# A five-stage decoder on one core: weights of three stages loaded, and of one rounded, a stage earlier, and one transfer per tile between stages

## The chip, the cores and the metric

The kernel runs on one core of a Trainium2 chip. The metric is the device time of the whole program in microseconds, as the median of the runs. The program is written in Bass: each engine (TensorE "PE", VectorE "DVE", ScalarE "ACT", GpSimd "POOL", SyncE "SP", which issues all transfers) has its own instruction stream, and the streams meet only at semaphores.

## What is computed

`x` is 2 sequences (B) of 2048 tokens (S) with 512 features (D). Six sublayers follow one another, each with a layer norm over the sum of its input and its output:

```
x = LN(x + delta_rule(x))            # 16 heads, short convolutions
x = LN(x + context_attention(x, c))  # 16 heads x 64, softmax over 128 context tokens
x = LN(x + ffn(x))                   # fake-quantised, below
x = LN(x + decaying_average(x))      # k, v, r products; running weighted average
x = LN(x + strided_attention(x, c))  # 16 heads over 8 strided context tokens each
x = LN(x + tree(x))                  # router products, 256 leaf probabilities, leaf values

def act_q(x, clip):  s = sigmoid(clip) * max|x| / 127; return clamp(round(x / s), -128, 127) * s
def w_q(w):          s = max|w| per row / 127;         return clamp(round(w / s), -128, 127) * s
def ffn(x):          xq = act_q(x, clip_x)
                     h = silu(xq @ w_q(gate).T) * (xq @ w_q(up).T)      # gate, up: 1408 x 512
                     return act_q(h, clip_down) @ w_q(down).T           # down: 512 x 1408
```

## The kernel before

The program runs five stages one after the other; every intermediate `x` lies in DRAM twice, as rows (`x`) and transposed, as columns (`xT`). `Memory`, the helper that owns a stage's buffers and semaphores, ends each stage with a barrier over all engines, so no instruction of a stage is issued before the stage ahead has stored everything.

- `delta_rule_attention`: not touched.
- `context_attention` (buffers `ctxatt_`): 16 steps of 128 tokens of both sequences, with a lag between the parts. In a step PE makes 8 units (2 heads each) of query products (L1249), scores (L1261), transposes of the probabilities (L1270), products with v (L1280), and then the output product (L1288) and the transposes of the new rows (L1295). DVE subtracts each row's maximum (`shift`, L1371 to L1374), ACT takes the exponential (L1330), DVE divides (`soften`, L1381 to L1383), ACT copies the transposed probabilities out of PSUM (L1335). SP's step is a fixed order of one column load, one row store, one row load and four column stores, each behind a wait.
- `quantised_feed_forward`, in three blocks. The hidden part (`ffnh_`) loads gate and up in four pieces, finds each row's maximum (L1569), scales (L1578, DVE), rounds by adding and taking away a large constant (L1665, ACT), clamps (L1583, DVE), transposes on PE (L1724), copies out of PSUM (`keep_piece`, L1673, ACT), and then runs over 8 tiles of 256 tokens of both sequences. Hidden values go to DRAM (`h`), since their scale needs the maximum over all of them. A short block (`ffns_`) turns the down weights. The last part (`ffnd_`) loads the hidden values again (L1826), scales them (L1872, DVE), rounds them, multiplies and norms.
- `decaying_average` (`wkv_`): 16 steps of 128 tokens, and `strided_attention_and_tree` (`tree_`), written out without loops. Both begin with the loads of their own weights.

What an engine does in a step is a Python function `step(n)`. `pipelined(...)` wraps it into a hardware loop, `unrolled(...)` writes all steps out. Transfers of SP are issued in program order, and a wait of SP holds up everything behind it:

```python
def step(n):                                   # SP, context_attention, before
    if n:
        wait(sp, projected, n, PAIRS // 2, -PAIRS // 2)
        ...
        sp.dma_start(xT_sb[:, n.parity]..., xT_view[n.slot()]...)                # L1184
    if t := n.back(LAG):
        wait(sp, norm.done, t, norm.OPS, norm.OPS)
        sp.dma_start(x_out_view[tokens(t)], new[:, t.parity])                    # L1190
    ...
    if t := n.back(LAG + 1):
        wait(sp, newT_kept, t, B, B)
        for k in range(KB):
            sp.dma_start(xT_out_view[:, k, :, tokens(t)], newT[:, t.parity, k])  # L1199
```

## Time and profile before

| | |
|---|---|
| median of 3 runs | 2984.55 us (2983.33 to 2997.24) |
| the profiled execution | 2985.33 us, of which the span of instructions is 2983.3 us |
| mean granted clock of TensorE | 0.939 of full speed |
| busy share of the span | PE 86%, PEld (weight loads) 61%, DVE 76%, ACT 48%, POOL 16% |
| moved | 233.95 MB, mean 78 GB/s |
| stage bounds (us from the span's start) | delta rule 0 to 1052.8, context attention to 1793.69, feed-forward hidden part to 2001, down weights turned by 2011.02, feed-forward last part to 2147.79, decaying average to 2698.76, strided attention and tree to 2983.3 |

The stage bounds are the starts of the first instructions behind each barrier in the timelines. Busy shares are means over stages with different limits: in the 740.89 us of context attention PE is busy for 703.64, in the first 30 us of the hidden part it is not busy at all. So each stage is read by itself, and for the start of a stage the timeline of its first microseconds on every engine.

In a row of the timeline the first number is the start (us from the span's start), the second the time from the first start to the last end of a run of like instructions, then engine, line, operation, out<-in by the names of the buffers, the shapes and the number of instructions (xN); in brackets stands how long the engine idled before the row, and what ended the idling. SPq is the time in which SP issues transfers.

### The profile page before, as it was taken

The page shows a single profiled execution, that of the slowest core. Times are in us where ns is not written, and L with a number is a line of the kernel's source. Part 1 is how long each engine was busy: PE and PEld are TensorE (multiplying, and loading weights), DVE is VectorE, ACT ScalarE, POOL GpSimd, SP SyncE. Part 2 cuts the span into 40 slices and gives each one's busy share as a digit, 9 for nine tenths or more (in the row PEclk, how much of TensorE's full clock was granted, in tenths as well). Part 3 has the DMA queues.
Part 4 walks back from the last instruction along what each step waited for, and adds up shares of the span by engine and source line. Part 5 has one row for each costly group of instructions (what it writes and reads, how often), then busy time and mean ns, then how long its engine had stood idle before and what let it go on. Part 6 is the DMA issues. An engine that isn't in the chain of part 4 may idle for free. (4 is left out here: it accounts for less than half of the span.)

```text
span 2983.3 us, 86333 instructions
## 1 busy us (share of the span) xinstructions
PE 2574.6 (86%) x35332; PEld 1821.6 (61%) x35332; DVE 2252.7 (76%) x3969; ACT 1422.2 (48%) x2560; POOL 484.5 (16%) x661
## 2 busy tenths in 40 slices
PE   7789888988886679999999974987589989987998
PEld 5667666766665357667676642443276766764665
DVE  4999998999988217787777856978578778760787
ACT  7666666666762102223222225545355565541444
POOL 2233223323421100000000000006400000000122
PEclk9899999999997689999999996999799999998999
DMA  2001110111010140111101116519821211214342
GB/s 84 24 11 37 48 39 32 39 46 39 32 46 25 45 170 8 50 57 57 56 29 55 49 51 214 188 67 337 279 69 57 85 56 56 77 36 163 113 128 78
DMA packets 184030, 233.95 MB, mean 78 GB/s; under 512 B 21778, under 2 KB 106386, under 8 KB 183700
## 3 DMA queue, kind: packets, MB, share of 16 engines
q1 hardware_dynamic: 183700, 229.17, 23.4%
q8 instruction: 253, 4.15, 0.6%
q14 instruction: 77, 0.63, 0.1%
HBM read 136.32 MB, written 92.81 MB: 77 GB/s over the span
## 5 line engine op out<-in xcount | busy, mean ns | idle before, releaser
L718 ACT ACTIVATE delta_product<-delta_line,delta_conv_w 128x256 f32<-128x256 f32 x576 | 247.2, 498 | 0.2
L1249 PE MATMUL ctxatt_banks<-ctxatt_xT,ctxatt_wq 128*128 128x256 f32 x1024 | 232.4, 380 | 2.9 <-ACT ctxatt_qT L1325 2.1
L1288 PE MATMUL ctxatt_banks<-ctxatt_wo,ctxatt_oT 128*128 128x512 f32 x512 | 229.4, 601 | 4.9 <-DVE ctxatt_norm_y L1394 4.9
L1249 PEld LDWEIGHTS ctxatt_banks<-ctxatt_xT,ctxatt_wq 128*128 128x128 f32 x1024 | 189.7, 190 | 28.4 <-ACT ctxatt_qT L1325 3.3
L944 DVE TENSOR_TENSOR delta_squares<-delta_t_sys 128x30 f32<-128x30 f32 (+14 forms) x480 | 185.7, 387 | 12.9
L947 DVE TENSOR_TENSOR delta_t_sys<-delta_t_sys,delta_squares 128x30 f32<-128x30 f32 (+14 forms) x480 | 161.4, 336 | 16.6
L1288 PEld LDWEIGHTS ctxatt_banks<-ctxatt_wo,ctxatt_oT 128*128 128x128 f32 x512 | 95.8, 192 | 116.0 <-issue 109.5
L1335 ACT ACTIVATE ctxatt_probsT<-ctxatt_banks 128x512 f32<-128x512 f32 x128 | 69.4, 594 | 203.3 <-PE ctxatt_banks L1270 203.3
L455 POOL TENSOR_TENSOR delta_product<-delta_product 128x1024 f32<-128x1024 f32 x48 | 127.4, 2655 | 233.7 <-ACT delta_product L718 233.7
L2169 PE MATMUL wkv_banks<-wkv_woT,wkv_oT 128*128 128x512 f32 x256 | 130.0, 667 | 38.0 <-DVE wkv_oT L2367 38.0
L884 DVE TENSOR_TENSOR delta_conv<-delta_conv,delta_product 128x1024 f32<-128x1024 f32 x96 | 133.6, 1404 | 17.1 <-ACT delta_product L718 12.5
L1325 ACT ACTIVATE ctxatt_qT<-ctxatt_banks 128x512 f32<-128x512 f32 x64 | 38.2, 597 | 226.7 <-PE ctxatt_banks L1249 226.7
L2159 PE MATMUL wkv_banks<-wkv_mixed,wkv_wkT 128*128 128x256 f32 x512 | 118.4, 385 | 27.8 <-DMA wkv_wrT<-L_attn_wrT 27.8
L710 ACT ACTIVATE delta_conv<-delta_line,delta_conv_b,delta_conv_w 128x256 f32<-128x256 f32 x192 | 111.0, 595 | 64.8 <-DVE delta_v_tok L895 61.3
L532 PE MATMUL delta_banks<-delta_xT,delta_wkT 128*128 128x256 f32 x512 | 132.7, 404 | 10.2 <-ACT delta_line L700 6.9
L595 PE MATMUL delta_banks<-delta_woT,delta_oT 128*128 128x512 f32 x256 | 130.2, 656 | 12.6 <-DVE delta_norm_y L1001 10.9
L1388 DVE COPY ctxatt_oT<-ctxatt_banks 128x512 f32<-128x512 f32 x64 | 44.1, 689 | 117.4 <-PE ctxatt_banks L1280 117.4
L532 PE MATMUL delta_banks<-delta_xT,delta_wqT 128*128 128x256 f32 x512 | 130.3, 400 | 0.2 <-ACT delta_line L700 0.2
L532 PE MATMUL delta_banks<-delta_xT,delta_wvT 128*128 128x256 f32 x512 | 127.7, 394 | 0.7 <-ACT delta_line L700 0.7
L2159 PEld LDWEIGHTS wkv_banks<-wkv_mixed,wkv_wkT 128*128 128x128 f32 x512 | 98.0, 194 | 41.3 <-DMA wkv_wrT<-L_attn_wrT 28.2
L2169 PEld LDWEIGHTS wkv_banks<-wkv_woT,wkv_oT 128*128 128x128 f32 x256 | 53.4, 214 | 107.8 <-issue 93.9
L209 POOL TENSOR_TENSOR ctxatt_norm_var_eps<-ctxatt_norm_moments,ctxatt_eps 128x2 f32<-128x2 f32 x16 | 3.1, 194 | 714.8 <-DVE ctxatt_norm_moments L193 714.8
(341 smaller groups left out, 6301.4 us busy)
## 6 DMA issues: line engine op xcount, KB each, us to landing
h<-ffn_hid SPq DMA_DIRECT2D x66, 256.0 KB, 2.0
ffn_hid<-h SPq DMA_DIRECT2D x6, 1536.0 KB, 9.6
wkv_xT<-xT SPq DMA_DIRECT2D x64, 129.0 KB, 2.8
delta_xT<-xT SPq DMA_DIRECT2D x16, 512.0 KB, 5.1
delta_x<-x SPq DMA_DIRECT2D x16, 512.0 KB, 3.7
xT<-delta_newT SPq DMA_DIRECT2D x16, 512.0 KB, 2.9
x<-delta_new SPq DMA_DIRECT2D x16, 512.0 KB, 3.9
ctxatt_xT<-xT SPq DMA_DIRECT2D x16, 512.0 KB, 4.3
```

The costliest lines, as they stand in the source:

```text
L455: pool.tensor_tensor(two_taps, two_taps, last, ALU.add).then_inc(paired, 1)
L532: mm = pe.matmul(b_proj[:, p % 2, 0:B * P], wT[NAMES[i]][:, k, g * P:(g + 1) * P], xT_sb[:, n.parity, k], start=k == 0, stop=k == KB - 1)
L595: mm = pe.matmul(b_out, oT[:, g, b * P:(b + 1) * P], woT[:, g], start=g == 0, stop=g == KB - 1)
L710: act.activation(conv[:, i, g].rearrange("p (b t) -> p b t", b=B), line[:, i, g, :, 0:P], ACT.Identity, bias=conv_b[:, i, g:g + 1], scale= ...
L718: made = act.activation(slot(n, i)[:, j - 1, g].rearrange("p (b t) -> p b t", b=B), line[:, i, g, :, j:j + P], ACT.Copy, scale=conv_w[:, i ...
L884: c.did(dve.tensor_tensor(total, total, slot(n, i)[:, half_of].rearrange("p g n -> p (g n)"), ALU.add))
L944: c.did(dve.tensor_tensor(parts, t_sys[:, j + 1:, j:j + 1].to_broadcast([P, rows, j]), t_sys[:, j:j + 1, 0:j].to_broadcast([P, rows, j]), ...
L947: c.did(dve.tensor_tensor(to, to, parts, ALU.add))
L1249: mm = pe.matmul(b_q[:, i * B * P:(i + 1) * B * P], wq[:, k, pair * P:(pair + 1) * P], xT_sb[:, n.parity, k], start=k == 0, stop=k == KB - 1)
L1288: mm = pe.matmul(b_o[:], oT[:, b, k, :], wo[:, k, :], start=k == 0, stop=k == PAIRS - 1)
L2159: mm = pe.matmul(bank(i, q)[:, j * WCOLS:(j + 1) * WCOLS], mats[name][:, k, u * P:(u + 1) * P], mixed[:, n.parity, i, k].rearrange("p b t ...
L2169: mm = pe.matmul(banks[:, OUT_BANK + r], oT[:, n.parity, k, r * P:(r + 1) * P], mats["woT"][:, k], start=k == 0, stop=k == KB - 1)
```

## The change

1. Gate and up weights are loaded and rounded during context attention, 22 blocks of 128 x 512 in 11 pieces of two. SP's `load_piece` opens its steps 1 to 11; DVE's `scale_piece` opens its steps 2 to 12 and `clip_piece` its steps 4 to 14; ACT's `round_piece` opens its steps 3 to 13. The rounded blocks, their scales, the identity matrix, the maxima of the rows and the first columns for the feed-forward stay in SBUF (`RoundedWeights`). Step 15 of SP loads these columns. The hidden part then begins with the 88 transposes, gate and up blocks in turn; ACT copies the gate blocks out of PSUM, DVE the up blocks.
2. The weights of the decaying average (4 of 1 MB and five short vectors) are loaded in step 1 of SP in the feed-forward's last part, its first columns in step 9 (`DecayWeights`).
3. The first weights of the last stage (4 of 1 MB, the context, a mask, the identity and four short vectors) are loaded in step 2 of SP in the decaying average (`AttentionWeights`).
4. `xT` between the stages has another layout, so that a tile's columns go in one transfer and not in four.
5. The loops of SP, PE, ACT and DVE in context attention and of PE in the decaying average are written out, and not hardware loops.

```diff
 # context_attention, SP
                 def step(n):
+                    if 1 <= n.index <= PIECES:
+                        load_piece(n.index - 1)
                     if n:
                         wait(sp, projected, n, PAIRS // 2, -PAIRS // 2)
...
                         sp.sem_inc(passed, 1)
-                        for k in range(KB):
-                            sp.dma_start(xT_out_view[:, k, :, tokens(t)], newT[:, t.parity, k]).then_inc(newT_stored[t.parity], 16)
-
-                pipelined(sp, STEPS, LAG + 1, step)
-                sp.wait_ge(topped, STEPS)
-                sp.dma_start(top_out, tops[:]).then_inc(top_stored, 16)
+                        to = xT_out[t.index // 2, :, :, :, (t.index % 2) * P:(t.index % 2 + 1) * P]
+                        sp.dma_start(to.rearrange("p k b t -> p (k b) t"), newT[:, t.parity].rearrange("p k b t -> p (k b) t")).then_inc(newT_stored[t.parity], 16)
+                    if n.index == STEPS - 1:
+                        load_first_columns()
+
+                unrolled(sp, STEPS, LAG + 1, step)
...
+                def load_piece(q):
+                    if q >= 2:
+                        sp.wait_ge(w_rounded, 2 * (q - 1))
+                    for i, (k, b) in enumerate(blocks(q)):
+                        sp.dma_start(raw[:, q % 2, i], later.w[k].rearrange("(b p) n -> p b n", p=P)[:, b]).then_inc(raw_here[q % 2], 16)
 # context_attention, ACT
+                def round_piece(q):
+                    for i, (k, b) in enumerate(blocks(q)):
+                        act.wait_ge(w_scaled, 2 * q + i + 1)
+                        act.activation(later.whole[k][:, b], raw[:, q % 2, i], ACT.Identity, bias=minus_magic[:]).then_inc(w_rounded, 1)
                 def step(n):
                     t1, t2, t3 = n.back(1), n.back(2), n.back(3)
+                    if 0 <= n.index - 3 < PIECES:
...
+                        round_piece(n.index - 3)
 # context_attention, DVE
                 def step(n):
                     t1, t2, t3 = n.back(1), n.back(2), n.back(3)
+                    if 0 <= n.index - 2 < PIECES:
+                        scale_piece(n.index - 2)
+                    if 0 <= n.index - 4 < PIECES:
+                        clip_piece(n.index - 4)
 # quantised_feed_forward, hidden part, DVE and ACT in step 0
                         if first:
                             scale_x(n)
-                            round_weights()
+                            scale_outputs()
+                            keep_turned(range(8))
                             clip_x(n)
+                            keep_turned(range(8, IB))
...
                         if first:
+                            keep_turned(range(4))
                             round_x(n)
-                            for q in range(len(PIECES)):
-                                round_piece(q)
-                                if q > 0:
-                                    keep_piece(q - 1)
-                            keep_piece(len(PIECES) - 1)
+                            keep_turned(range(4, IB))
 # last part, SP
+                        if isinstance(n.index, int) and n.index == 1:
+                            decay.load(sp, decay_here)
+                        if isinstance(n.index, int) and n.index == FSTEPS + 1:
+                            sp.wait_ge(zero_stored, 16)
+                            sp.wait_ge(newT_stored[KEPT % 2], 16 * (KEPT // 2 + 1))
+                            decay.load_first_columns(sp, xT_out, decay_here)
 # decaying_average, SP and PE
+                    if isinstance(n.index, int) and n.index == 2:
+                        later.load(sp, later_here)
...
-                pipelined(pe, WSTEPS, LAG, step, 2)
+                unrolled(pe, WSTEPS, LAG, step)
```

The new functions that DVE calls at the start of its steps of context attention:

```python
def scale_piece(q):
    if q == 0:
        dve.wait_ge(wo_here, 32)
        dve.tensor_copy(later.identb[:], ident[:]).then_inc(ident_made, 1)
    dve.wait_ge(raw_here[q % 2], 32 * (q // 2 + 1))
    ...                                   # for both blocks: maximum, / 127, reciprocal, then
        dve.tensor_scalar(raw[:, q % 2, i], raw[:, q % 2, i], raw_inv[:, i:i + 1], MAGIC, ALU.mult, ALU.add).then_inc(w_scaled, 1)

def clip_piece(q):
    dve.wait_ge(w_rounded, 2 * q + 2)
    for k, b in blocks(q):
        dve.tensor_scalar(later.whole[k][:, b], later.whole[k][:, b], QMAX, -QMAX - 1.0, ALU.min, ALU.max).then_inc(w_clipped, 1)
```

On SP, steps 4 and 5 of context attention before, as they stand ahead of the hardware loop, which repeats the same transfers (the names are buffers of the stage; `x` and `xT` lie in DRAM; waits are not shown):

```order
L1184 DMA ctxatt_xT<-xT 128x1024
L1190 DMA x<-ctxatt_new 128x2x512
L1194 DMA ctxatt_x<-x 128x2x512
L1199 DMA xT<-ctxatt_newT 256x1x128 x4
L1184 DMA ctxatt_xT<-xT 128x1024
L1190 DMA x<-ctxatt_new 128x2x512
```

The same place now:

```order
L1194 DMA ctxatt_raw<-L_ffn_gate 128x512 x2
L1207 DMA ctxatt_xT<-xT 128x1024
L1213 DMA x<-ctxatt_new 128x2x512
L1217 DMA ctxatt_x<-x 128x2x512
L1222 DMA xT<-ctxatt_newT 1024x1x128
L1194 DMA ctxatt_raw<-L_ffn_gate 128x512 x2
L1207 DMA ctxatt_xT<-xT 128x1024
```

Four column stores have become one, and the two loads of weight blocks, with their wait for the rounding of the piece that lay in the same buffer, stand ahead of the column load.

On DVE, the start of a step of context attention before, between the last divisions of the step ahead and the copies of the next output:

```order
L1381 TENSOR_REDUCE ctxatt_den<-ctxatt_probs 128x8
L1382 RECIPROCAL ctxatt_den<-ctxatt_den 128x8
L1383 TENSOR_TENSOR ctxatt_probs<-ctxatt_probs,ctxatt_den 128x1024
L1371 TENSOR_TENSOR ctxatt_scores<-ctxatt_banks,ctxatt_bias 128x1024
L1373 TENSOR_REDUCE ctxatt_top<-ctxatt_scores 128x8
L1374 TENSOR_TENSOR ctxatt_scores<-ctxatt_scores,ctxatt_top 128x1024
L1388 COPY ctxatt_oT<-ctxatt_banks 128x512
```

And the same place of a step now:

```order
L1411 TENSOR_REDUCE ctxatt_den<-ctxatt_probs 128x8
L1412 RECIPROCAL ctxatt_den<-ctxatt_den 128x8
L1413 TENSOR_TENSOR ctxatt_probs<-ctxatt_probs,ctxatt_den 128x1024
L1462 TENSOR_REDUCE rounded_gate_scale<-ctxatt_raw 128x1 x2
L1465 TENSOR_SCALAR rounded_gate_scale<-rounded_gate_scale 128x1 x2
L1468 RECIPROCAL ctxatt_raw_inv<-rounded_gate_scale 128x1 x2
L1471 TENSOR_SCALAR ctxatt_raw<-ctxatt_raw,ctxatt_raw_inv 128x512 x2
L1476 TENSOR_SCALAR rounded_whole_gate<-rounded_whole_gate 128x512 x2
L1401 TENSOR_TENSOR ctxatt_scores<-ctxatt_banks,ctxatt_bias 128x1024
L1403 TENSOR_REDUCE ctxatt_top<-ctxatt_scores 128x8
L1404 TENSOR_TENSOR ctxatt_scores<-ctxatt_scores,ctxatt_top 128x1024
L1418 COPY ctxatt_oT<-ctxatt_banks 128x512
```

Ten instructions on weight blocks now stand ahead of the shift of the step's first unit.

On SP, the start of the feed-forward's last part before (`h` is the hidden values in DRAM):

```order
L1819 DMA xT<-ffnd_zero 256x1x1 x4
L1831 DMA ffnd_x<-x 128x2x512 x2
L1826 DMA ffn_hid<-h 128x6x512
L1826 DMA ffn_hid<-h 128x5x512
L1831 DMA ffnd_x<-x 128x2x512 x2
```

And now:

```order
L1859 DMA xT<-ffnd_zero 1024x1x1
L1871 DMA ffnd_x<-x 128x2x512 x2
L2037 DMA decay_mix<-L_attn_mix_k 128x4x1
L2037 DMA decay_mix<-L_attn_mix_v 128x4x1
L2037 DMA decay_mix<-L_attn_mix_r 128x4x1
L2038 DMA decay_decay<-L_attn_decay 128x4x1
L2039 DMA decay_first<-L_attn_first 128x4x1
L2041 DMA decay_wkT<-L_attn_wkT 128x4x512
L2041 DMA decay_wvT<-L_attn_wvT 128x4x512
L2041 DMA decay_wrT<-L_attn_wrT 128x4x512
L2041 DMA decay_woT<-L_attn_woT 128x4x512
L1866 DMA ffn_hid<-h 128x6x512
```

Nine loads for the next stage stand ahead of the first load of hidden values (tile 2; tiles 0 and 1 never left SBUF).

## Rows read from the trace of the kernel before

**Rows 1.** Windows: bounds, length; busy PE, PEld, DVE, ACT, POOL; clock; DMA; GB/s.

```profile
1052.80:1793.69 740.89, 703.64 (x4328) 494.01 (x4328) 521.81 (x606) 188.99 (x289) 14.50 (x35) 0.98 0.18 58
2020.00:2120.00 100.00, 86.28 (x421) 43.20 (x419) 87.37 (x136) 48.78 (x38) 68.76 (x42) 0.95 1.04 349
2147.79:2698.76 550.97, 480.08 (x1920) 360.83 (x1920) 406.67 (x674) 308.49 (x577) 41.45 (x183) 0.93 0.23 69
```

**Rows 2.** Timelines of PE, DVE and ACT at the hidden part's start.

```profile
1793.70 1.28 ACT L1658 ACT_TABLE_LOAD   x1 [5.61 <-PEq L130]
1803.31 1.29 DVE L1608 TENSOR_SCALAR ffnh_xT<-ffnh_xT,ffnh_x_inv 128x2048 f32<-128x2048 f32 x1 [2.85 <-DMA ffnh_xT<-xT]
1808.11 2.82 DVE L1569 TENSOR_REDUCE ffnh_gate_scale<-ffn_hid 128x5 f32<-128x2560 f32 x1 [3.51 <-DMA ffn_hid<-L_ffn_gate]
1811.39 2.07 DVE L1578 TENSOR_SCALAR ffn_hid<-ffn_hid,ffnh_gate_inv 128x512 f32<-128x512 f32 x5
1811.91 3.17 ACT L1665 ACTIVATE ffnh_whole_gate<-ffn_hid,ffn_minus_magic 128x512 bf16<-128x512 f32 x5 [5.22 <-DVE ffn_hid L1578]
1820.45 2.31 PE L1724 MATMUL ffn_banks<-ffn_identb,ffnh_whole_gate 128*128 128x128 bf16 x20 [33.00 <-DVE ffnh_whole_gate L1583]
1834.46 5.43 ACT L1673 ACTIVATE ffnh_upT<-ffn_banks 128x512 bf16<-128x512 bf16 x11
1839.94 1.04 PE L1737 MATMUL ffn_banks<-ffnh_xq,ffnh_gateT 128*128 128x512 bf16 x4 [1.56 <-ACT ffnh_upT L1673]
```

**Rows 3.** Timelines of PE and SP at the decaying average's and the tree's start.

```profile
2155.48 4.90 ACT L2211 ACTIVATE wkv_mixed<-wkv_xT,wkv_mix 128x256 f32<-128x256 f32 x12 [6.41 <-DMA wkv_xT<-xT]
2164.92 6.29 PE L2159 MATMUL wkv_banks<-wkv_mixed,wkv_wkT 128*128 128x256 f32 x16 [27.82 <-DMA wkv_wrT<-L_attn_wrT]
2708.67 9.22 PE L2600 MATMUL tree_banks<-tree_cT,tree_wkT 128*128 128x256 f32 x32 [17.35 <-DMA tree_wkT<-L_wkT]
```

**Rows 4.** Timelines of DVE, ACT and PE in context attention, around a step's start.

```profile
1424.75 1.22 DVE L1374 TENSOR_TENSOR ctxatt_scores<-ctxatt_scores,ctxatt_top 128x1024 f32<-128x1024 f32 x1
1429.99 0.69 DVE L1388 COPY ctxatt_oT<-ctxatt_banks 128x512 f32<-128x512 f32 x1 [4.01 <-PE ctxatt_banks L1280]
1430.59 0.68 DVE L1394 TENSOR_TENSOR ctxatt_norm_y<-ctxatt_banks,ctxatt_x 128x512 f32<-128x512 f32 x1
1429.43 1.05 ACT L1330 ACTIVATE ctxatt_probs<-ctxatt_scores 128x1024 f32<-128x1024 f32 x1
1139.41 2.08 PE L1261 MATMUL ctxatt_banks<-ctxatt_kT,ctxatt_qT 64*128 64x128 f32 x16 [2.23 <-DVE ctxatt_scores L1371]
```

**Rows 5.** Context attention: SP, ACT, PE timelines; landings of ctxatt_xT, then of ctxatt_x.

```profile
1446.22 0.35 SPq L1184 DMA_DIRECT2D ctxatt_xT<-xT  x1
1457.71 0.60 ACT L1343 ACTIVATE ctxatt_newT<-ctxatt_banks 128x512 f32<-128x512 f32 x1
1466.54 3.62 PE L1249 MATMUL ctxatt_banks<-ctxatt_xT,ctxatt_wq 128*128 128x256 f32 x16
DMA to landing us min/median/max: 3.2/4.3/14.8
DMA to landing us min/median/max: 4.2/4.6/4.8
```

**Rows 6.** SP's stores at the ends of three stages.

```profile
1790.74 0.61 SPq L1203 DMA_DIRECT2D top<-ctxatt_tops  x1
2134.81 6.41 SPq L1841 DMA_DIRECT2D xT<-ffnd_newT  x8
2692.04 2.52 SPq L2077 DMA_DIRECT2D xT<-wkv_newT  x4
```

**Rows 7.** The last part's hidden loads: SP and DVE timelines, and the page's issues.

```profile
2091.02 3.88 SPq L1826 DMA_DIRECT2D ffn_hid<-h  x2
2105.25 1.79 DVE L1872 TENSOR_SCALAR ffn_hid<-ffn_hid,ffn_h_inv 128x3072 f32<-128x3072 f32 x1
ffn_hid<-h SPq DMA_DIRECT2D x6, 1536.0 KB, 9.6
```

More of the change, by code:

```diff
@@ L1102, with context_attention @@
 MASKED = -1e30
-def context_attention(nc, x_in, xT_in, ctxT, weights, consts, x_out, xT_out, top_out):
+def context_attention(nc, x_in, xT_in, ctxT, weights, consts, x_out, xT_out, later):
     w = weights
@@ L1450, with __init__, quantised_feed_forward @@
 FROWS = FCOLS // P
-def quantised_feed_forward(nc, x_in, xT_in, top_in, weights, consts, h_dram, x_out, xT_out):
+class RoundedWeights:
+    def __init__(self, nc, ctx, w):
+        m = Memory(nc, ctx, "rounded")
+        self.w = w
+        self.whole = {k: m.sbuf(f"whole_{k}", [P, IB, D], BF16) for k in ("gate", "up")}
+        self.scale = {k: m.sbuf(f"{k}_scale", [P, IB]) for k in ("gate", "up")}
+        self.ident = m.sbuf("ident", [P, P])
+        self.identb = m.sbuf("identb", [P, P], BF16)
+        self.clip = m.sbuf("clip", [P, 2])
+        self.tops = m.sbuf("tops", [P, S // P])
+        self.xT = m.sbuf("xT", [P, KB * FCOLS])
+def quantised_feed_forward(nc, x_in, xT_in, weights, consts, h_dram, x_out, xT_out, later, decay):
     w = weights
@@ L1968, with __init__, tile, reserve @@
 LN_SHIFT = 60
-def decaying_average(nc, x_in, xT_in, weights, consts, x_out, xT_out):
-    w = weights
+class DecayWeights:
+    def __init__(self, nc, ctx, w):
+        self.nc, self.ctx, self.w = nc, ctx, w
+    def tile(self, name, shape):
+        return self.ctx.enter_context(self.nc.sbuf_tensor(f"decay_{name}", shape, F32, side="right"))
+    def reserve(self):
+        self.mats = {k: self.tile(k, [P, KB, D]) for k in ("wkT", "wvT", "wrT", "woT")}
+        self.mix = self.tile("mix", [P, 3, KB])
+        self.decay, self.first = self.tile("decay", [P, KB]), self.tile("first", [P, KB])
+        self.xT = self.tile("xT", [P, KB, B, WT + 1])
+        self.LOADS = 3 + 2 + 4 + 1
+    def load(self, sp, here_):
+        w = self.w
+        with self.nc.allow_non_contiguous_dma(reason="columns of five vectors, once"):
+            for i, k in enumerate(("mix_k", "mix_v", "mix_r")):
+                sp.dma_start(self.mix[:, i], w[k].rearrange("a b (k p) -> p (a b k)", p=P)).then_inc(here_, 16)
+            sp.dma_start(self.decay[:], w["decay"].rearrange("(k p) -> p k", p=P)).then_inc(here_, 16)
+            sp.dma_start(self.first[:], w["first"].rearrange("(k p) -> p k", p=P)).then_inc(here_, 16)
+        for k in ("wkT", "wvT", "wrT", "woT"):
+            sp.dma_start(self.mats[k][:], w[k].rearrange("(k p) n -> p k n", p=P)).then_inc(here_, 16)
+    def load_first_columns(self, sp, xT, here_):
+        sp.dma_start(self.xT[:].rearrange("p k b t -> p (k b) t"), xT[:, :, :, 0:WT + 1].rearrange("p k b t -> p (k b) t")).then_inc(here_, 16)
+def decaying_average(nc, x_in, xT_in, pre, later, x_out, xT_out):
     LAG = 3
@@ L2172, in turn_new @@
                 def turn_new(n, r, now):
+                    if n.index == 0 and r == 0:
+                        pe.wait_ge(later_here, 16 * later.LOADS)
                     wait(pe, norm.finished, n, WROWS, r + 1)
```

326 lines of the change are left out of this document (158 added, 168 removed).

## The prediction

> **What bounds the kernel now.** I read the page for the shares, then the windows by stage, then the timelines of all engines around each stage's start and inside a steady step of context attention and of the feed-forward's last part. No engine is the bound of the whole. Context attention belongs to PE: 703.64 of 740.89 us [rows 1]. The decaying average does so less strictly (480.08 of 550.97), and the feed-forward's last part to DVE and the DMA engines together: in 2020 to 2120 DVE is busy for 87% and the DMA share is 1.04 at 349 GB/s [rows 1]. Between the stages stand stretches in which PE does nothing, since a stage's first loads are issued only behind the barrier. At the hidden part's start (S = 1793.69) PE idles 33.00 us until the first rounded piece, and makes its first product at 1839.94, 46.25 us after S [rows 2]. The decaying average (S = 2147.79) makes its first product at 2164.92, 17.1 us after S, and the tree (S = 2698.76) at 2708.67, 9.9 after S, both released by loads of weights [rows 3]. These three starts are 73 us, and the question is how much of them goes and what the moved work costs where it now stands.
>
> **The hidden part's start: -35.3.** What is left after S, from the rows of the same operations: ACT loads its table (1.28), takes the sigmoid (0.2, estimated), and two short DVE operations follow at about 0.23 each (the two between the reduction's end at 1810.93 and 1811.39 took 0.46 together) [rows 2]: S+1.95. The scaling of the first tile takes 1.29 [rows 2]: S+3.2, two short operations S+3.6 at most, I take 3.4. PE has been transposing since S, 20 in 2.31 us, so 88 in 10.2 at most [rows 2]; ACT's copies out of PSUM are 5.43/11 = 0.49 each [rows 2], 11 of them and the rounding of the tile of 2048 (four times 3.17/5 = 0.63 for 512 [rows 2], less the overhead of three: 2 us, estimated) end by S+9.1. DVE is last: 11 copies from PSUM. The trace has none in bf16; the nearest is the fp32 copy of 512, 0.69 us with its successor 0.60 after it [rows 4]. At 0.60: 8 copies to S+8.2, the clamp of the tile (0.7, estimated from DVE's rows of 2048 elements at half the bytes), 3 copies to S+10.7, first product at S+10.9. 46.25 - 10.9 = 35.3. Bounds: at half of 0.60 the chain ends at S+7.4 and PE, with its transposes, decides: S+9.3, which is 1.6 less; if DVE's and ACT's copies and PE slow one another down, S+14, 3 more. The maximum over partitions on POOL ran ahead of these rows and in the shadow of loads before; if it is slow, it delays x_inv: 0 taken, +5 as a bound. The Trainium skill, VectorE: DVE Perf Modes, section Why PSUM operands drop a tier, says that an operand in PSUM allows the packed 16-bit mode at most and none for fp32; by that the bf16 copies could go at half of the fp32 row's time and the sum would be 1.6 us lower; no row here shows such a copy on DVE.
>
> **Context attention, what moves in.** DVE gets per step two maxima of 512 (2.82/5 = 0.56 each), four short operations (0.23), two scalings (2.07/5 = 0.41) and two clamps (0.2, bf16 in SBUF) [rows 2]: 3.3 us, 11 times. They stand ahead of the first shift of the step. DVE idles 4.01 us behind that shift, waiting for PE, before L1388 [rows 4], and the exponential that needs the shift starts at 1429.43 when the shift ended at 1425.97: 3.46 us of slack [rows 4]. 3.3 fit, with 0.2 to spare: 0 taken; if the blocks take 4 us, 0.5 in each of 11 steps, 6 us. In step 2 there is no such slack: PE already waits 2.23 us for the shift's bank at 1139.41 [rows 4], and the first scaling (2.9 with no clamp yet) and the cast of the identity (0.2) stand ahead of it: +3.1, bounds 0 and 5. ACT gets two roundings at 0.63, PE nothing, the DMA engines 5.8 MB in a stage with a share of 0.18 [rows 1].
>
> SP's wait matters more. The load of piece q waits until ACT has rounded piece q-2, which ACT does at the beginning of the same step, so behind its last copy of the step ahead: 1457.71 + 0.60 = 1458.31 [rows 5], two roundings to 1459.65, two weight loads issued by 1460.4 (0.35 a transfer [rows 5]), and the column load, until now issued at 1446.22, at about 1460.95. PE needs it at 1466.54 [rows 5]. The landing of columns has a median of 4.3 us, but behind 512 KB of other transfers the row load's 4.2 to 4.8 is the nearest [rows 5]: landed at 1465.55, 1.0 to spare. 0 taken; bound: 1.1 us in each of the nine steps with this wait, 10 us. Writing the loops out puts nothing on PE's path.
>
> **Context attention's tail: -1.8.** The four column stores and the store of the maxima, which is issued at 1790.74 + 0.61 [rows 6], become one issue, about 2.6 us earlier at its end, of which the landing gives 0.8 back.
>
> **The last part: +5.** The weights of the decaying average, 4.19 MB, stand ahead of the hidden values in a queue that is full: at 349 GB/s 12.0 us of transfers [rows 1], and about 1.5 for the five vectors of single numbers. The DVE chain has slack against it: the last hidden tile was issued at 2091.02 with 3.88 for its two halves, lands 9.6 after issue, about 2101 to 2104, and is needed at 2105.25 [rows 7]; I take 4.5 us of slack at the end. The stage's start stores zeros in one transfer and not four, at 0.80 us an issue (6.41/8 [rows 6]) 2.4 us. 13.5 - 4.5 - 2.4 = 6.6; a part of the load lies in gaps before tile 2 is due: 5 taken, bounds 0 (all in gaps) and 13.5 (none).
>
> **Stores and starts behind it.** The last part's tail: 8 column issues of 0.80 become 2 [rows 6], and of the 4.8 us about half was on the path: -2.3. The decaying average's start: table load 1.28 [rows 2], four shares at 4.90/12 = 0.41 [rows 3], the mix 0.5: S+3.5 and not S+17.1: -13.6. The attention weights, 5.3 MB, fall into a stage with a DMA share of 0.23 [rows 1]: 0. Its tail: 4 issues, 2.52, become one [rows 6]: -1.9. The tree's start: first product at S+0.3 and not S+9.9: -9.6; the loads left to it are needed only behind the 32 products of 9.22 us [rows 3] and the score products, +3 as a bound.
>
> **The sum.** -1.8 - 35.3 + 3.1 + 0 + 5 - 2.3 - 13.6 - 1.9 - 9.6 = -56.4 against the profiled execution's 2985.3, of which 2983.3 are span: 2929. That execution is 0.8 above the median of the runs, which is within rounding of the sum.
>
> The new column layout gives DRAM rows of one partition 64 KB apart in the last hand-over. The Trainium skill, DMA: Bandwidth & Descriptors, section Latency and other measured facts, gives 207 GB/s for a pitch of 512 KiB and less above it; 64 KB is below what it measured, no row here has such a pitch, and the sum is made without it; by 207 GB/s a store of 0.5 MB would take 2.5 us, an estimate of 1 us more at a tail.
>
> **Rivals.**
> 1. *The column load comes late behind SP's wait, each step.* For it: the 1.0 us of slack worked out above is smaller than the spread of landings (3.2 to 14.8 [rows 5]). Against it: the row load never took over 4.8. At 6 to 8 us of landing PE waits 0.4 to 2.4 us, nine times, and DVE's chain then slips too: 4 to 30 us, 2940 to 2960.
> 2. *The last part is saturated and pays in full*: 13.5 and not 5: 2937. For it the share of 1.04; against it the slack at tile 7.
> 3. *Slower.* The same load, landing 13 us after issue or later: 1460.95 + 13 - 1466.54 = 7.4 us in each of nine steps is 67, more than the gain; from about 13.5 us on the kernel is over 0.5% slower. The longest landing seen is 14.8 [rows 5], once; the median of 4.3 speaks against it. At 14.8: 2929 + 9 x 9.3 = 3013.
> 4. *The starts don't shrink*: something hidden behind the loads (the maximum on POOL, table loads) takes their time, and the moved work costs some us a step: 2975 to 2985.
>
> **Chances.** Forecast 0.68, with a range of its own of 2918 to 2940 (hidden in full with fast copies 2921; C's upper half 2937); rival 1 0.15; rival 2 0.1; rival 3 0.03; rival 4 0.04. About 0.5% is what a measurement of this kernel can tell from no change (15 us): faster 0.93, same 0.04, slower 0.03. The range holds the forecast, rival 2 and half of rival 1: 2916 to 2950.
>
> **What would show it.** In the profile after: first feed-forward product 9 to 12 us behind the barrier, that of the decaying average at 3 to 5, that of the tree under 1. Context attention as long as before, less 1.8, plus 3; PE's idle time before L1249's line by DMA would be rival 1. The last part 3 us longer, with DVE waiting for hidden values at tile 2 and 7. It would be wrong if the column load's landing grows past 5.6 us, if DVE's blocks take over 3.5 us a step, or if PE, no longer idle at a start, is granted another clock; that I can't price from rows.

## The result and the profile after

The changed kernel takes 2943.98 us (median of 4 runs, 2942.35 to 2950.99), the one before 2983.94 (4 runs): 0.986 of its time, interval 0.9839 to 0.9881, so 40 us less. 2929 was forecast, with a range of 2916 to 2950. The profiled execution took 2942.35, of which 2940.3 are span. A second measurement gave 2945.72 and 0.9865 (0.9847 to 0.9884).

The windows of the profile after, in the columns of [rows 1]: the hidden part and the down weights, the last part, 100 us inside it, and the decaying average.

```profile
1793.16:1982.40 189.24, 166.09 (x830) 82.22 (x844) 148.34 (x236) 93.98 (x125) 1.03 (x6) 0.96 0.41 146
1982.40:2128.55 146.15, 99.41 (x472) 52.54 (x480) 103.64 (x160) 58.67 (x49) 67.86 (x50) 0.88 0.99 324
1990.00:2090.00 100.00, 80.12 (x385) 40.32 (x393) 80.53 (x123) 43.96 (x33) 54.07 (x36) 0.94 1.05 358
2128.55:2665.65 537.10, 483.02 (x1920) 361.63 (x1920) 406.98 (x674) 308.59 (x577) 41.83 (x183) 0.94 0.23 72
```

The last part has grown: in [rows 1] DVE was busy for 87% of a 100 us stretch, here for 80.5%, at the same DMA share (1.05). The table sets the terms of the prediction against the lengths between the same instructions in three profiled executions. "Again" is the changed kernel's second profile. The first product of context attention, ahead of which nothing was changed, starts anywhere from 1053.9 to 1062.3 us over the profiles, so stages are compared by length. A length of one profile has a scatter of its own: see the last part, below.

| stretch | predicted | before | after | again |
|---|---|---|---|---|
| context attention, first product to first output product | +3.1 | 95.80 | 96.89 | 98.53 |
| from there to the last output product | 0 | 618.82 | 617.53 | 618.93 |
| from there to the barrier | -1.8 | 20.74 | 20.56 | 19.88 |
| barrier to first feed-forward product | -35.3 | 46.24 | 18.29 | 16.88 |
| down weights' maximum to the last transposes of the last part | +5 | 130.81 | 140.24 | 140.80 |
| from there to the barrier | -2.3 | 14.37 | 14.49 | 14.87 |
| barrier to the decaying average's first product | -13.6 | 17.13 | 3.62 | 3.77 |
| its last transposes to the tree's first product | -11.5 | 19.32 | 8.75 | 8.73 |

Against the 56.4 us of the forecast the two spans, 2940.3 and 2943.9, are short by 13 and 17 us. Two terms carry 11 to 12 of them: the start of the hidden part (28.0 to 29.4 gained, not 35.3) and the last part (9.4 to 10.0 paid, not 5).

The timelines of DVE, POOL and PE at the hidden part's start, after:

```profile
1793.20 0.17 DVE L1622 TENSOR_REDUCE ffnh_top<-rounded_tops 128x1 f32<-128x16 f32 x1 [7.90 <-PEq L130]
1793.26 0.21 POOL L1613 MEMSET ffn_ones<- 128x128 f32 x1
1802.61 0.38 POOL L1615 PARTITION_ALL_REDUCE ffnh_top_all<-ffnh_top  x1 [9.14 <-issue]
1803.02 0.16 DVE L1625 SCALAR_TENSOR_TENSOR ffnh_x_scale<-ffnh_top_all,rounded_clip 128x1 f32<-128x1 f32 x1 [9.64 <-POOL ffnh_top_all L1615]
1804.88 1.74 DVE L1653 COPY ffnh_upT<-ffn_banks 128x512 bf16<-128x512 bf16 x5
1811.45 0.81 PE L1776 MATMUL ffn_banks<-ffnh_xq,ffnh_gateT 128*128 128x512 bf16 x3 [0.78 <-ACT ffnh_gateT L1717]
```

POOL's maximum over partitions has its input at 1793.37 and starts at 1802.61. "issue" says that nothing that the profile shows was awaited. DVE's copies behind it go faster than forecast: five bf16 copies from PSUM take 1.74 us, 0.33 apart and not 0.60. What releases the first product is ACT's last copy. The clock, which the prediction could not price, brings no term to the products: PE is granted 0.50 of it in most of the transposes (1793.2 to 1796.0, 1805.0 to 1808.0) and 1.00 from the first product on, as in the kernel before (0.50 until 1839.0, 1.00 from 1840.0).

The last part, after. Of DVE's timeline only the three rows that end a wait for hidden values, and then SP's at the start:

```profile
2008.90 1.82 DVE L1918 TENSOR_SCALAR ffn_hid<-ffn_hid,ffn_h_inv 128x3072 f32<-128x3072 f32 x1 [3.44 <-DMA ffn_hid<-h]
2067.89 1.82 DVE L1918 TENSOR_SCALAR ffn_hid<-ffn_hid,ffn_h_inv 128x3072 f32<-128x3072 f32 x1 [3.01 <-DMA ffn_hid<-h]
2085.86 1.82 DVE L1918 TENSOR_SCALAR ffn_hid<-ffn_hid,ffn_h_inv 128x3072 f32<-128x3072 f32 x1 [4.61 <-DMA ffn_hid<-h]
```

```profile
1984.38 0.46 SPq L2037 DMA_DIRECT2D decay_mix<-L_attn_mix_k  x1
...
1987.97 1.73 SPq L2039 DMA_DIRECT2D decay_first<-L_attn_first  x1
1989.74 0.51 SPq L2041 DMA_DIRECT2D decay_wkT<-L_attn_wkT  x1
```

The three waits are 11.06 us; before, tile 7 was taken at 2105.25 without one [rows 7]. The five vectors alone hold SP from 1984.38 to 1989.74.

The length of the last part can be read in six profiles in which it is the same: the two of the table and, from the experiments below, those of e1_pool_warm, e2_down_later, e6_dve_maxima and e8_pool_last. They give 140.24, 140.80, 143.16, 140.92, 140.34 and 141.54 us. So one profile tells it to about 3 us, and the change cost 9.4 to 12.4 against the single profile of before.

Context attention, after: DVE, ACT, SP and PE around a step's start, and the landings of the columns.

```profile
1139.56 2.08 PE L1285 MATMUL ctxatt_banks<-ctxatt_kT,ctxatt_qT 64*128 64x128 f32 x16 [4.98 <-DVE ctxatt_scores L1401]
...
1423.17 1.27 DVE L1462 TENSOR_REDUCE rounded_up_scale<-ctxatt_raw 128x1 f32<-128x512 f32 x2
...
1426.19 1.22 DVE L1401 TENSOR_TENSOR ctxatt_scores<-ctxatt_banks,ctxatt_bias 128x1024 f32<-128x1024 f32 x1
...
1428.69 1.23 DVE L1404 TENSOR_TENSOR ctxatt_scores<-ctxatt_scores,ctxatt_top 128x1024 f32<-128x1024 f32 x1
1430.81 0.69 DVE L1418 COPY ctxatt_oT<-ctxatt_banks 128x512 f32<-128x512 f32 x1 [0.90 <-PE ctxatt_banks L1304]
1430.27 1.05 ACT L1354 ACTIVATE ctxatt_probs<-ctxatt_scores 128x1024 f32<-128x1024 f32 x1
1461.40 0.36 SPq L1207 DMA_DIRECT2D ctxatt_xT<-xT  x1
1467.46 3.62 PE L1273 MATMUL ctxatt_banks<-ctxatt_xT,ctxatt_wq 128*128 128x256 f32 x16
DMA to landing us min/median/max: 3.3/4.7/13.4
```

The weight work on DVE takes 3.02 us (1423.17 to 1426.19; 3.3 forecast), the idle time of 4.01 [rows 4] has shrunk to 0.90, and PE goes on as before. The column load is issued at 1461.40 (1460.95 forecast) and used at 1467.46 with no wait on PE. In the steps with weight loads that have a landing on record, columns take 4.2 to 4.8 us; later ones take 5.9 to 6.0, but are issued earlier in the step. The two starts behind it, on PE:

```profile
2132.17 6.47 PE L2218 MATMUL wkv_banks<-wkv_mixed,decay_wkT 128*128 128x256 f32 x16 [14.59 <-DVE wkv_mixed L2370]
2665.70 9.39 PE L2670 MATMUL tree_banks<-attention_cT,attention_wkT 128*128 128x256 f32 x32 [6.78 <-PEq L130]
```

Neither is released by a transfer any more, as both were in [rows 3].

### The profile page after: what moved, and what is told of

It reads as the page before. It is cut to its first block and busy times, and to the rows that moved or that the text cites. A ratio compares the mean times of both kernels' runs of the same rounds, so it can differ in the third digit from the quotient of the medians.

```text
span 2940.3 us, 85155 instructions
## 1 busy us (share of the span) xinstructions
PE 2571.4 (87%) x35310; PEld 1821.1 (62%) x35332; DVE 2263.1 (77%) x4052; ACT 1418.3 (48%) x2549; POOL 475.2 (16%) x662
## 5 line engine op out<-in xcount | busy, mean ns | idle before, releaser
L2226 PE MATMUL wkv_banks<-decay_woT,wkv_oT 128*128 128x512 f32 x256 | 132.8, 679 | 35.4 <-DVE wkv_oT L2426 35.4
L2218 PE MATMUL wkv_banks<-wkv_mixed,decay_wkT 128*128 128x256 f32 x512 | 118.6, 386 | 14.6 <-DVE wkv_mixed L2370 14.6
L2226 PEld LDWEIGHTS wkv_banks<-decay_woT,wkv_oT 128*128 128x128 f32 x256 | 54.3, 218 | 107.1 <-issue 64.8
L1354 ACT ACTIVATE ctxatt_probs<-ctxatt_scores 128x1024 f32<-128x1024 f32 x64 | 67.4, 1052 | 102.4 <-DVE ctxatt_scores L1404 102.4
L2218 PE MATMUL wkv_banks<-wkv_mixed,decay_wvT 128*128 128x256 f32 x512 | 115.8, 379 | 0.0
```

The costliest lines, as they stand in the source:

```text
L2218: mm = pe.matmul(bank(i, q)[:, j * WCOLS:(j + 1) * WCOLS], mats[name][:, k, u * P:(u + 1) * P], mixed[:, n.parity, i, k].rearrange("p b t ...
L2226: mm = pe.matmul(banks[:, OUT_BANK + r], oT[:, n.parity, k, r * P:(r + 1) * P], mats["woT"][:, k], start=k == 0, stop=k == KB - 1)
```

## The experiments

All are edits of the changed kernel. "Length of the last part" is the stretch from the down weights' maximum to the last transposes: 130.81 before, 140.24 and 140.80 in the changed kernel, and up to 143.16 where only other stages are edited.

**POOL's maximum run once ahead (e1_pool_warm).**

```diff
                         norm.root(pool, t, eps, half)
+                    if isinstance(n.index, int) and n.index == STEPS:
+                        pool.partition_all_reduce(warm[:], half[:, 0:1], P, bass.bass_isa.ReduceOp.max)
```

> The changed kernel with one more maximum over partitions on POOL, of a constant and read by nobody, put into the last steps of context attention, 20 us ahead of the hidden part. In the changed kernel the maximum that the hidden part needs starts 9.4 us behind the barrier, although its input is ready 0.2 us behind it. Theory A (what it waits for is the fetch of the instruction's own code, which the first use brings in and a later one finds there): it starts within 0.6 us of the barrier, the first feed-forward product comes 9 to 11 us behind it and not 18.3, and the kernel takes about 2936, 8 less than the changed kernel. Theory B (the wait belongs to the start of a block, or is that of the barrier, whatever was used before): the maximum still starts 9 us behind the barrier and the kernel takes 2944.

2944.57 us, and the maximum starts 9.4 us behind the barrier as before. POOL's timeline, e1_pool_warm:

```profile
1765.32 0.38 POOL L1244 PARTITION_ALL_REDUCE ctxatt_warm<-ctxatt_half  x1 [5.73 <-issue]
1781.86 0.19 POOL L209 TENSOR_TENSOR ctxatt_norm_var_eps<-ctxatt_norm_moments,ctxatt_eps 128x2 f32<-128x2 f32 x1 [16.16 <-DVE ctxatt_norm_moments L193]
...
1801.72 0.38 POOL L1618 PARTITION_ALL_REDUCE ffnh_top_all<-ffnh_top  x1 [9.06 <-issue]
```

Theory A falls: a first use is not what costs. Both uses pay, 5.73 in the last steps of context attention and 9.06 at the barrier, and both follow plain POOL operations.

**The down weights loaded a step later (e2_down_later).**

```diff
-                        second = isinstance(n.index, int) and n.index == 1
+                        third = isinstance(n.index, int) and n.index == 2
```

> The changed kernel with the 2.9 MB load of the down weights issued in SP's third step of the hidden part and not in its second, so that the DMA engines are nearly free in the first 5 us behind the barrier. Theory A1 (the fetch on POOL waits behind the transfers of the down weights): the maximum starts 3 to 6 us behind the barrier and not 9.4, and the kernel takes 2938 to 2941. Theory A2 (a first use costs about 9 us whatever the DMA engines do): it still starts 9 us behind the barrier, 2944.

2945.10 us; the maximum starts 7.81 us behind the barrier and the first product comes at 16.26. With the load ahead nine profiles show 8.1 to 9.5. So at most a small part is given back and theory A1's 3 to 6 us are not reached. Nor does the DMA share put the waits in order: in e2_down_later it is 0.41 over the 7.50 us of idle time ahead of the maximum, in e1_pool_warm 0.57 over the 5.73, and 0.87 over its 9.06; in the kernel before, behind the same barrier, 0.32 over 5.68. Whether and how transfers lengthen the wait stays open.

**The maximum with no other kind of operation before it (e8_pool_last).** One unused maximum ends POOL's part of context attention, and the four fills of the hidden part stand behind its maximum.

```diff
                 pipelined(pool, STEPS, LAG, step, 2)
+                pool.partition_all_reduce(warm[:], half[:, 0:1], P, bass.bass_isa.ReduceOp.max)
...
-                    pool.memset(minus_magic[:], -MAGIC).then_inc(ready, 1)
-                    pool.memset(half[:], -0.5)
...
                     pool.partition_all_reduce(top_all[:], top[:], P, bass.bass_isa.ReduceOp.max).then_inc(topped, 1)
+                    pool.memset(minus_magic[:], -MAGIC).then_inc(ready, 1)
```

> The changed kernel with a maximum over partitions, of a constant and read by nobody, as POOL's last operation of context attention, and in the hidden part the maximum ahead of POOL's four fills, so that no other kind of POOL operation stands between the two. So far: the maximum that the hidden part needs started 5.7 us behind the fills in the kernel before, 7.5 to 9.1 in five runs of the changed one and its variants, also where one had run 36 us earlier with two products on POOL between them (9.1), and only 0.5 us behind its input where the operation before it on POOL was the same kind (the down weights' part). Theory G (POOL pays 6 to 9 us each time it goes from its plain operations to this one): it now starts under 1 us behind the barrier, the first feed-forward product comes 9 to 11 us behind it and not 17.2, and the kernel takes about 2937. Theory H (the wait belongs to the start behind a long block or barrier): it starts 7 to 9 us behind the barrier again, 2944.

2936.96 us, 0.9832 (0.9809 to 0.9856). POOL and PE, e8_pool_last:

```profile
1790.94 0.38 POOL L1245 PARTITION_ALL_REDUCE ctxatt_warm<-ctxatt_half  x1 [5.57 <-issue]
1795.15 0.35 POOL L1613 PARTITION_ALL_REDUCE ffnh_top_all<-ffnh_top  x1 [3.84 <-DVE ffnh_top L1624]
...
1804.24 0.81 PE L1778 MATMUL ffn_banks<-ffnh_xq,ffnh_gateT 128*128 128x512 bf16 x3 [1.55 <-ACT ffnh_gateT L1719]
```

Theory G holds: the change of kind costs 5.57 us where nobody waits, and the maximum follows its input by 0.1. The first product comes 9.4 us behind the barrier, which is the prediction's bound for fast copies (9.3). What ends last is not PE's transposes, as in that bound, but ACT's copies, the releaser in the row; they end 9.1 us behind the barrier, as the prediction has them. The start of the hidden part gains 7.5 to 8.9 us against the changed kernel's two profiles; the totals differ by 7 to 8.8.

**The decaying average's weights behind the hidden values (e3_decay_late).**

```diff
-                        if isinstance(n.index, int) and n.index == 1:
+                        if isinstance(n.index, int) and n.index == FSTEPS:
                             decay.load(sp, decay_here)
```

> The changed kernel with the decaying average's weights loaded in SP's ninth step of the feed-forward's last part, when all hidden values are loaded, and not in its second. The last part took 136.8 us before and 146 in the changed kernel. Theory C (it is short of transfers, and 4.2 MB ahead of the hidden values are paid nearly in full as waits of DVE in tiles 2, 6 and 7): the waits of DVE for hidden values go, the last part takes 136 to 138 and the kernel about 2935. Theory D (the 9 us come from the new layout of the column stores, of 1024 rows in one transfer): nothing changes, 2944.

2949.21 us, 3.5 to 5.2 above the changed kernel's two medians. The length of the last part is 130.37, as before the change, so theory D falls; but from the last transposes to the barrier it now takes 29.17 and not 14.5 to 14.9. SP and DVE, e3_decay_late:

```profile
2078.37 1.82 DVE L1918 TENSOR_SCALAR ffn_hid<-ffn_hid,ffn_h_inv 128x3072 f32<-128x3072 f32 x1 [0.67 <-DMA ffn_hid<-h]
...
2087.43 4.95 SPq L2037 DMA_DIRECT2D decay_mix<-L_attn_mix_k  x1
...
2098.66 0.51 SPq L2041 DMA_DIRECT2D decay_wkT<-L_attn_wkT  x1
```

The compute gets its 10 us back and the stores lose 14.5: SP sits on the five vectors for 11.2 us (2087.43 to 2098.66), and the new rows and columns queue behind them and the matrices. Theory C is right on the place and wrong on the sum: it expected 2935.

**One matrix in each of four steps (e4_decay_spread).**

```diff
-                        if isinstance(n.index, int) and n.index == 1:
-                            decay.load(sp, decay_here)
+                        if isinstance(n.index, int) and 1 <= n.index <= 4:
+                            decay.load(sp, decay_here, n.index - 1)
```

> The changed kernel with the four matrices of the decaying average loaded one in each of SP's steps 1 to 4 of the last part, and not all in step 1. Theory C (bytes): as long as in the changed kernel, the last part 145 to 148. Theory J (it is the burst of 4.2 MB ahead of the first hidden values that costs): the last part 138 to 141.

2945.5 us in one run; length 142.71. Theory J, which needs the last part shorter by 5 to 8 us, falls: the burst is not what costs.

**Only the first matrix in the last part (e9_one_matrix).**

```diff
-        for k in ("wkT", "wvT", "wrT", "woT"):
-            sp.dma_start(self.mats[k][:], w[k]...).then_inc(here_, 16)
+        sp.dma_start(self.mats["wkT"][:], w["wkT"]...).then_inc(here_, 16)
...
+                        pre.load_others(sp, others_here)      # SP, decaying average, step 0
...
+                    if n.index == 0 and q == 0 and i > 0:
+                        pe.wait_ge(others_here[i - 1], 16)
```

> The changed kernel with only the first matrix (1 MB) of the decaying average and its five vectors loaded in the feed-forward's last part; the other three are loaded at the start of the decaying average, each awaited by its first product. Theory C (the last part is bound by what it transfers, and each MB costs 3 us of it): it takes 3.1 MB / 349 GB/s = 9 us less than the changed kernel's 146, about 137 to 139. The second and third matrices are needed 9.9 and 13.4 us behind the barrier and land about 5 and 8 us behind it, so the decaying average loses nothing: about 2936. Theory I (not the bytes but the five vectors of single numbers ahead of the hidden values cost the time): the last part stays at 143 or more, 2942 to 2944.

2942.62 us. The length is 134.46, so three matrices are 5.8 to 6.3 us by the changed kernel's own two profiles, 2 for each MB, and 8.7 by the longest of the six, which is nearly the 3 of theory C. At the start of the decaying average DVE and PE now wait:

```profile
2143.29 1.68 DVE L2379 SCALAR_TENSOR_TENSOR wkv_mixed<-wkv_xT,wkv_rest,wkv_mixed 128x256 f32<-128x256 f32 x4 [2.68 <-ACT wkv_mixed L2278]
2174.38 9.72 PE L2235 MATMUL wkv_banks<-decay_woT,wkv_oT 128*128 128x512 f32 x16 [5.92 <-DVE wkv_oT L2435]
```

The columns of the second tile stood behind all three matrices, and the first output product waited 5.92 us; it waits 3.03 in the changed kernel. What the stage as a whole loses by that is not shown: from its first product to its last transposes it takes 524.54 us here, and 521.05 to 524.78 in the six profiles in which it is the same.

**Only the vectors moved (e11_vectors).** They are loaded in SP's third step of the hidden part.

```diff
+                        if isinstance(n.index, int) and n.index == 2:
+                            decay.load_vectors(sp, vectors_here)
```

> The changed kernel with only the five vectors of the decaying average (512 single numbers each) loaded in the hidden part; the four matrices stay in step 1 of the last part. In the changed kernel their issue takes SP 5.4 us there. Theory C (the bytes of the matrices cost the time): the last part from the down weights' part to its last transposes takes 139 to 142 as so far. Theory I (the vectors cost a good part of it, with their thousands of four-byte pieces): 136 or less, and the kernel about 2940.

2945.19 us against 2945.72 for the changed kernel beside it, whose runs differ by 13, so the totals say nothing; the length is 137.26, between what the two theories expected, and 3.0 to 3.5 less than in the changed kernel's two profiles (5.9 less than the longest of the six). DVE, e11_vectors:

```profile
2006.38 1.82 DVE L1922 TENSOR_SCALAR ffn_hid<-ffn_hid,ffn_h_inv 128x3072 f32<-128x3072 f32 x1 [0.57 <-DMA ffn_hid<-h]
2064.72 1.82 DVE L1922 TENSOR_SCALAR ffn_hid<-ffn_hid,ffn_h_inv 128x3072 f32<-128x3072 f32 x1 [2.35 <-DMA ffn_hid<-h]
2083.20 1.82 DVE L1922 TENSOR_SCALAR ffn_hid<-ffn_hid,ffn_h_inv 128x3072 f32<-128x3072 f32 x1 [5.13 <-DMA ffn_hid<-h]
```

The first of the three waits goes from 3.44 (2.89 to 4.02 in the six profiles) to 0.57, the other two stay: the first belongs to the vectors, which stand ahead of tile 2, the others to the matrices. Both theories hold a part: about a third of the loss is 10 KB in single numbers. The trace shows how they are moved: from 1800 to 1830 us e11_vectors has 2816 packets of 4 bytes, in the changed kernel 176, so 2640 more for 2560 numbers. They take 1.5 us of the 16 DMA engines, the prediction's figure. What costs more is SP, which issues them: without them tile 2's load is issued 6.9 us behind the barrier and not 10.2, 3.3 earlier.

**Four stores a tile again (e5_four_stores).** In three stages, into the new layout.

```diff
-                        sp.dma_start(to.rearrange("p k b t -> p (k b) t"), newT[...]...).then_inc(newT_stored[t.parity], 16)
+                        for k in range(KB):
+                            sp.dma_start(to[:, k], newT[:, t.parity, k]).then_inc(newT_stored[t.parity], 16)
```

> The changed kernel with the column stores of context attention, of the feed-forward's last part and of the decaying average issued as four transfers a tile again, into the new layout. Theory E (of the prediction: at a stage's end the issue of the stores lies on the path): context attention ends 1.8 us later, the last part 2.3, the decaying average 1.9, the kernel takes 2950. Theory F (what ends a stage is the time that the descriptors of the last tile take on the DMA engines, the same in one transfer as in four): each stage ends within 0.8 us of the changed kernel's, 2944 to 2946.

2947.37 us. The three stage ends are 19.94, 15.14 and 8.77 against 20.56, 14.49 and 8.75 (19.88, 14.87 and 8.73 in the second profile): theory F, all within 0.7. The length of the last part was 143.24, no more than the 143.16 of e1_pool_warm, in which the last part is the changed kernel's; so a cost of the four issues there is neither shown nor excluded. Issues and landings, the changed kernel:

```profile
xT<-ctxatt_newT SPq DMA_DIRECT2D x2, 512.0 KB, 4.4
xT<-ffnd_newT SPq DMA_DIRECT2D x3, 1024.0 KB, 9.4
```

and e5_four_stores:

```profile
xT<-ctxatt_newT SPq DMA_DIRECT2D x8, 128.0 KB, 2.2
xT<-ffnd_newT SPq DMA_DIRECT2D x12, 256.0 KB, 6.9
```

What is saved at the issue comes back as a longer landing.

**DVE's maxima three times (e6_dve_maxima).**

```diff
-                    for i, (k, b) in enumerate(blocks(q)):
-                        w.did(dve.tensor_reduce(...))
+                    for again in range(3):
+                        for i, (k, b) in enumerate(blocks(q)):
+                            w.did(dve.tensor_reduce(...))
```

> The changed kernel with the two maxima of each piece taken three times on DVE, which makes the work ahead of the first shift of a step 2.6 us longer, 11 times. In the changed kernel that work takes 3.02 us, the shift behind it ends 0.35 us ahead of the exponential, and DVE idles 0.90 us behind it. Theory K (of the prediction: only the idle time behind the shift covers it): 1.7 to 2.3 us in each of ten steps and 2.6 at the first, context attention 19 to 26 us longer. Theory L (lags between the engines cover more than one step's idle time): under 8 us.

2954.86 us in one run. The start of context attention is 3.4 us longer (101.89 against 98.53), but from the first to the last output product it takes 620.70 against 618.93: 1.8 us in ten steps. Theory L holds. DVE, e6_dve_maxima:

```profile
1408.52 1.00 DVE L204 TENSOR_SCALAR ctxatt_new<-ctxatt_norm_y,ctxatt_norm_moments,ctxatt_norm_rstd 128x512 f32<-128x512 f32 x2 [1.08 <-POOL ctxatt_norm_rstd L211]
1425.87 0.69 DVE L1418 COPY ctxatt_oT<-ctxatt_banks 128x512 f32<-128x512 f32 x1 [1.76 <-PE ctxatt_banks L1304]
```

These are the only waits left in the step. In the kernel before there were two more, behind the step's first two shifts: the 4.01 us of [rows 4] and, on DVE,

```profile
1436.48 0.69 DVE L1388 COPY ctxatt_oT<-ctxatt_banks 128x512 f32<-128x512 f32 x1 [1.56 <-PE ctxatt_banks L1280]
```

They are gone, 5.57 us together, which is what 3.02 + 2.6 needs.

**Together (e10_together).** e8_pool_last, the vectors in the hidden part, one matrix in the last part, two at the start of the decaying average and the fourth behind the second tile's columns.

```diff
+                        pre.load_others(sp, (("wvT", others_here[0]), ("wrT", others_here[1])))   # step 0
...
+                    if isinstance(n.index, int) and n.index == 1:
+                        pre.load_others(sp, (("woT", others_here[2]),))
```

> The changed kernel with four things: POOL's maximum as in e8_pool_last; the five vectors of the decaying average loaded in SP's third step of the hidden part; in the last part only its first matrix; the second and third matrix loaded at the start of the decaying average, and the fourth behind the columns of its second tile (in e9_one_matrix those columns came behind all matrices, and DVE waited 2.68 us for shares of them, PE 5.92 and not 3.03 for its first output product). By the runs so far: 7 to 8 less than the changed kernel by POOL's maximum, 7 to 9 in the last part, nothing back in the decaying average: 2928 to 2930. If the bytes of the last part are paid elsewhere (the decaying average's start), 2933 to 2937.

2926.50 us (5 runs, 2924.03 to 2930.97), 0.9795 (0.9782 to 0.9809) of the kernel before and 19 us less than the changed kernel beside it. DVE and PE, e10_together:

```profile
2074.31 1.82 DVE L1924 TENSOR_SCALAR ffn_hid<-ffn_hid,ffn_h_inv 128x3072 f32<-128x3072 f32 x1 [0.81 <-DMA ffn_hid<-h]
```

```profile
2161.79 7.11 PE L2248 MATMUL wkv_banks<-decay_woT,wkv_oT 128*128 128x512 f32 x16 [3.13 <-DVE wkv_oT L2448]
```

The hidden part's first product comes at 9.18, the last part's length is 131.38, and the first output product waits 3.13. Against "again" that is 7.7 us by the hidden part's start and 9.4 by the last part, 17 of the 19; nothing is paid back in the decaying average. 2928 to 2930 was expected, so the median is 1.5 us below it.

**The base (e12_after_again).**

> The changed kernel itself once more, as a base for the two others on the same chip: 2942 to 2946. The delta rule's end, which no change touches, has varied from 1053.9 to 1061.6 us over the runs so far; so stages are compared by their lengths, and the totals only to about 4 us.

2945.72 us (4 runs, 2941.18 to 2953.95).

## Why the prediction was right, and where it was off

The direction held and the time fell into the stated range; the gain was 40 us and not 56. Point by point:

- *The starts of the decaying average and of the tree* were right: 3.62 to 3.77 us (3.5 forecast) and 0.05 (0.3 forecast). *Rival 4* came only in the hidden part, for some 7 of its 35 us.
- *The hidden part's start* was off by 6 to 7.3 us, and the step that failed is "The maximum over partitions on POOL ran ahead of these rows and in the shadow of loads before; if it is slow, it delays x_inv: 0 taken, +5 as a bound". The trace of before had it in a row of POOL that was not set against the new order. The maximum there follows its fills by 5.68 us too, but it also starts 0.46 behind the end of its input, so the profile names the input:

```profile
1799.68 0.38 POOL L1553 PARTITION_ALL_REDUCE ffnh_top_all<-ffnh_top  x1 [5.68 <-DVE ffnh_top L1562]
```

It is a cost of its own, which holds the maximum until 7.8 to 9.5 us behind the barrier in the changed kernel, shown by e8_pool_last, which removes it. The bound of +5 was too low as well.
- In the same term *the copies out of PSUM* were sized at 0.60 and took 0.33 each. By the Trainium skill, VectorE: DVE Perf Modes, section Why PSUM operands drop a tier, 16-bit operands in PSUM may go at the packed mode; the trace agrees (0.42 for one of 512, and 0.69 in fp32 [rows 4]). It shows in e8_pool_last, where the product comes at 9.4 and not at 10.9, and ACT and not DVE is last. The bound of 9.3 was put down to PE's transposes, for which the prediction's own working gives up to 10.2; the term that holds is ACT's 9.1, and that 9.3 and 9.4 agree is in part luck.
- *Context attention* was right: 0 in the steady steps, and 1.1 to 2.7 at its start (3.1 forecast; 2.4 to 3.0 in the variants that leave DVE's part alone). But "3.3 fit, with 0.2 to spare" was wrong as a margin: e6_dve_maxima put 2.6 us more there for 1.8 us in all, since the idle time behind the second shift counts as well.
- *Rival 1 and rival 3* (the column load late behind SP's wait) did not come. The issue time was forecast to 0.45 us, the landing's median rose from 4.3 to 4.7, and the longest landing (13.4) is the one at the stage's start.
- *The last part* was mis-sized, 5 for 9.4 to 10.0 (to 12.4 with the scatter of the six profiles). Rival 2 had the mechanism, and its price of 13.5 was too high, by little if the longest profile is taken. The five vectors were "about 1.5" and are 3.0 to 3.5 (e11_vectors, and e10_together against e9_one_matrix: 134.46 - 131.38 = 3.1). The matrices are 6.5 (137.26 - 130.81), of which the first has 0.6 and the other three 5.9; these are differences of single profiles, and the split is no better than their scatter. The saving of 2.4 by the single store of zeros was subtracted as if it lay on the path; its issue went from 2.61 to 0.57 us, but no run shows it on the path.
- *The ends of stages* failed as a step: "they become one issue", -1.8, -2.3 and -1.9, were -0.2 to -0.9, +0.1 to +0.5 and -0.7. Nor do the last part's 8 column issues become 2, as the prediction has it, but one, at 2118.30. Of the decaying average's 19.32 - 8.75 = 10.6 us, 9.9 are the tree's start. The transfers, not their issues, end a stage (e5_four_stores).

That the median stayed in the range is in part luck: the range reached to 2950 for the sake of the rivals. The forecast's own range ended at 2940, and the median lies 4 us above it.

The sum by what was measured in the second profile: 2.7 + 0.1 - 0.9 - 29.4 + 10.0 + 0.5 - 13.4 - 10.6 = -41.0, against 39.4 between the spans of that profile (2943.9) and of before. The rest lies ahead of context attention's first product, which comes 2.4 us later, and inside the long loops.

## What to carry to other kernels

A load that is moved into a stage with a full DMA queue is not free: its price is what the queue can't take, and it can be split by need, as here, where a stage needs its first matrix at once and its last 40 us later. When waits are removed from a stage's start, look at every engine's first operation there, since the one that was hidden behind the loads is next; a row whose releaser came just before it may be waiting for something else. Work that is moved in is covered by all the idle times up to where the next engine is due, and not only by the nearest one.

## What was not expected of the hardware

- POOL pays for going from its plain operations (fills, products) to the maximum over partitions: 5.57 to 5.73 us in context attention (e1_pool_warm, e8_pool_last, e10_together) and behind the fills of the kernel before, 7.50 to 9.14 behind those of the changed kernel. With no plain operation between two of them the second follows its input by 0.1. What it does in that time no run shows.
- Five loads of 512 single numbers, 10 KB, cost 3.0 to 3.5 us of a stage whose DMA queue is full, about half as much as 4.2 MB of matrices, and hold SP for 5.4 to 11.2 us there. By the Trainium skill, DMA: Bandwidth & Descriptors, section Rules for kernel authors, a last dimension that is not contiguous becomes one descriptor for each element; the trace agrees, with the 2640 packets of 4 bytes for 2560 numbers.
